# Attention sums on TensorE: products stored side by side, and matrix rows 2 and 3 summed there too

## Chip, core and metric

The kernel runs on one NeuronCore of a Trainium2 chip. The metric is the device time of one execution in microseconds (us), the median of several runs. The engines are TensorE (PE in the rows, with its weight loads apart as PEld), VectorE (DVE), ScalarE (ACT), GpSimd (POOL) and the DMA queues (SP). They work in parallel and wait for each other through semaphores.

## What is computed

An audio tower: seven 1-d convolutions with layer norm and GELU over 64 clips, a projection to 12 positions of 192 numbers a clip, one attention block and one mixture of experts. The change touches the attention alone, whose reference is, cut to what matters:

```python
sim1 = jnp.einsum('bhnd,bhmd->bhnm', q, k_landmarks)      # same for sim2, sim3
attn1 = jax.nn.softmax(sim1, axis=-1)                     # and attn2, attn3
z = jnp.swapaxes(x, -1, -2) / (jnp.max(col) * jnp.max(row))
for _ in range(iters):                                    # 6 times, x = attn2
    xz = x @ z
    z = 0.25 * z @ (13.0 * I - xz @ (15.0 * I - xz @ (7.0 * I - xz)))
out = attn1 @ (attn2_inv @ (attn3 @ v))
```

There are 64 clips x 12 heads. The 12 positions are padded to 64 landmarks; since all pads are alike the kernel keeps them as one extra row, so each head's matrix is 13 x 13 (`R` is 13, `SEQ` 12), and the iteration is rewritten so that only products of symmetric results are left, two of them an iteration.

## The kernel before

The attention puts one clip and one half of the heads on each of the 128 partitions ("lanes"): a partition holds 6 heads (`HL`) with their small matrices, so a matrix product is no TensorE matmul. It is a multiplication of a row, spread over all columns, with the other matrix (13 x 13 x 6 heads = 1014 words a partition), followed by a sum over the inner index. A `RowSums` job describes one such product and says who does which row. In order the program does: `scoring` (q times k, 16 terms a sum), softmax and norms, `valuing` (attention matrix times v, 12 terms), `outer` (13 terms), then in a hardware loop of `PINV_ITERS` = 6 iterations `squaring` and `closing` (13 terms each), and last `applying` (13 terms). A job's rows go three ways:

- `sum_pe`: VectorE multiplies them into `for_pe` (L1211) and TensorE sums them: one matmul a term, with the identity as weights, that adds into the same PSUM columns (L1037). In the trace each of these fp32 matmuls stands as two records. ScalarE copies the sums out (L1123), for the symmetric products also to the mirrored place. `sum_pe_pool` are rows that GpSimd multiplies into `pool_for_pe` (L1086) for the same treatment, in a second batch.
- `by_vector`: VectorE multiplies into `rowt` (L1225) and sums (L1229) itself.
- `by_pool`: GpSimd multiplies into `from_pool` (L1089), VectorE sums (L1233).

Symmetric products skip what the mirror gives: row i is computed from column i on, and ScalarE copies it to the column (L1118). For a loop product rows 0 and 1 are `sum_pe`, rows 2 and 3 `by_vector`, rows 4 to 12 `by_pool`. The first operand of VectorE's products is read from PSUM: rows 0 and 1 where TensorE summed them, others after ScalarE brought them there (L1135).

Each job ends in a wait of VectorE for all its row sums and copies; ScalarE's next copies and GpSimd's next products wait for the same. Between the two products of an iteration VectorE forms `c4` (L1313); GpSimd waits for it. No scheduler moves anything: each engine's order is as written.

Two other kinds of matmul matter for the prediction because of how they read: the convolutions (L562, fp32, 400 columns) read their input with a step of 2 words (8 bytes), since their stride is 2; the experts' matmuls (L1438, 384 columns, a 4-byte type that is one record a matmul) read contiguous words.

The layout in `for_pe` is by term: `p (k n)`, all columns n of term k in one run, so VectorE writes a product's inner index with a step of the batch's width (156 words for rows 0 and 1 of a 13 x 13 product) and TensorE reads each term as one contiguous run.

Of the kernel before, what the change touches and what calls it, by code (L numbers as in the profile page):

```python
# [32 lines left out]
P = 128  # L33
# [735 lines left out]
class RowSums:  # L769


    def __init__(self, terms, width, sum_pe, sum_pe_pool, by_vector, by_pool, near, first, second, out, bank=0, mirror=None):
        self.batches = [rows for rows in (sum_pe, sum_pe_pool) if rows]
        self.terms, self.width, self.bank = terms, width, bank
# [13 lines left out]
    def by_term(self, buffers, i):  # L788

        batch = next(n for n, rows in enumerate(self.batches) if i in rows)  # L790
        places, wide = self.places(self.batches[batch])
        full = buffers[batch][:, 0:self.terms * wide].rearrange("p (k n) -> p k n", k=self.terms)[:, :, places[i]]
        return full.rearrange("p k (a b) -> p a b k", a=self.first(i).shape[1])

    def copies(self, bank, rows):

        places, wide = self.places(rows)
        if self.mirror:
            last = len(rows)
            both = bank[:, 0:wide].rearrange("p (i h j) -> p i h j", i=last, h=self.first(0).shape[1])  # L800
            whole, below = self.mirror(None)
            yield whole, both.rearrange("p i h j -> p h i j")
            yield below, both[:, :, :, last:].rearrange("p i h j -> p h i j")
            return
# [6 lines left out]
    def copied(self):  # L811

        batch = list(self.sum_pe) + list(self.sum_pe_pool)
        return (2 if self.mirror else len(batch)) + len(self.mirrors())


class Before:


    def __init__(self, jobs=0, sums=0, reduced=0, copied=0, pooled=0):  # L820
        self.jobs, self.sums, self.reduced, self.copied, self.pooled = jobs, sums, reduced, copied, pooled

    def after(self, *jobs, times=1):
        add = lambda f: sum(f(j) for j in jobs)
        return Before(self.jobs + len(jobs) * times, self.sums + add(lambda j: len(j.batches)) * times, self.reduced + add(lambda j: len(j.reduced)) * times,
# [31 lines left out]
def attention(nc, io, res, top):  # L857
# [33 lines left out]
    with ExitStack() as ctx:  # L891
# [13 lines left out]
        pool_for_pe = sb("pool_for_pe", [P, 2 * HL * R * DH])  # L905
# [11 lines left out]
        wv = sb("wv", [P, HL, R, DH])  # L917
# [13 lines left out]
        mat_row = lambda x: x.rearrange("p (h k) -> p h k", k=R)  # L931
        q_near = near_rows([bank(3, 0), bank(3, 1)], 3, HL * DH, lane_row)
# [3 lines left out]
        scoring = RowSums(DH, lambda i: HL * SEQ, [0, 1], [6, 7], [2, 3, 4, 5], [8, 9, 10, 11],  # L936
# [697 lines left out]
```

## Time and profile before

| | |
|---|---|
| median of 3 runs | 1031.38 us (1031.18 to 1031.56) |
| the profiled execution | 1027.13 us, its span on the core 1025.3 us |
| convolutions | to about 550 us of the span |
| attention | about 550 to 865 us, of it the loop 673.5 to 828 us |
| experts | from 865 us on |

The profile is of one execution. A line of the timeline has its start in us from the span's start, its length in us (of the whole group when x2 or more instructions are merged), the engine, the line of the kernel, the operation with out<-in, the shape, and in brackets the idle time of the engine ahead of it with what ended it. "PEclk" or the number behind the busy times in a row by windows is TensorE's granted clock as a share of 2.4 GHz; 0.50 is 1.2 GHz.

### The profile page before, as it was taken

Reading aid. Unit: us, or ns where it says so; the run is one execution under the profiler, and the core shown is the slowest. Engines: PE = TensorE matmul, PEld = TensorE weight load, DVE = VectorE, ACT = ScalarE, POOL = GpSimd, SP = SyncE. Lnnn points to the kernel's source line nnn. Section 1 sums busy time; section 2 is a strip of 40 time slices with the busy share of each in tenths; the row PEclk is TensorE's granted clock in tenths of the full one; section 3 lists DMA queues with packets and bytes.
Section 4 is the critical chain, followed back from the end, with each engine's and each line's share of the span. In section 5 each row is a group of like instructions: output and inputs, shape, how many; then the busy total and the mean of one; then the engine's idle time right before and its main releaser. Section 6 shows DMA issues by size and latency. Waiting matters only on the chain. (4 is left out here: it accounts for less than half of the span.)

```text
span 1025.3 us, 10797 instructions
## 1 busy us (share of the span) xinstructions
PE 744.8 (73%) x3517; PEld 530.8 (52%) x3517; DVE 644.1 (63%) x1479; ACT 269.6 (26%) x463; POOL 201.4 (20%) x199
## 2 busy tenths in 40 slices
PE   0089998999799989999962570544444464899999
PEld 0036654665465645665642460444444453899965
DVE  4818566866485552455554579999999996522243
ACT  0043354334433443433221020022222211133100
POOL 2000000000000000000000055546666682033000
PEclk9999997999698988998965586766666677699999
DMA  1430500050003300000003500000000000000000
GB/s 53 70 87 20 112 1 1 1 112 20 2 0 53 68 0 1 1 1 1 1 0 91 125 1 0 0 1 0 0 0 0 0 0 1 0 1 1 1 1 23
DMA packets 22663, 21.73 MB, mean 21 GB/s; under 512 B 17036, under 2 KB 21196, under 8 KB 21388
## 3 DMA queue, kind: packets, MB, share of 16 engines
q1 hardware_dynamic: 22620, 21.20, 9.7%
q8 instruction: 22, 0.36, 0.2%
q14 instruction: 21, 0.17, 0.1%
HBM read 17.51 MB, written 3.66 MB: 21 GB/s over the span
## 5 line engine op out<-in xcount | busy, mean ns | idle before, releaser
L562 PE MATMUL ps<-h,w 128*128 128x400 f32 x720 | 290.8, 548 | 1.6 <-ACT h L630 1.5
L562 PEld LDWEIGHTS ps<-h,w 128*128 128x128 f32 x720 | 139.3, 200 | 105.9 <-issue 103.2
L1037 PE MATMUL pt<-for_pe,ident 128*128 128x156 f32 (+2 forms) x420 | 99.3, 418 | 107.8 <-DVE for_pe L1211 107.8
L1037 PEld LDWEIGHTS pt<-for_pe,ident 128*128 128x128 f32 x420 | 91.5, 280 | 115.5 <-DVE for_pe L1211 111.9
L722 DVE COPY h<-ps 128x800 f32<-128x800 f32 (+2 forms) x58 | 56.5, 975 | 94.4 <-PE ps L562 93.6
L575 PEld LDWEIGHTS ps<-averager,sq 128*100 128x100 f32 (+2 forms) x1024 | 99.5, 172 | 23.1 <-ACT sq L623 19.3
L575 PE MATMUL ps<-averager,sq 128*100 128x1 f32 (+2 forms) x1024 | 100.0, 228 | 8.9 <-ACT sq L623 8.4
L623 ACT ACTIVATE sq<-h 128x800 f32<-128x800 f32 (+2 forms) x58 | 49.8, 858 | 174.5 <-DVE h L722 174.5
L753 DVE TENSOR_TENSOR h<-h,ps 128x400 f32<-128x400 f32 (+2 forms) x116 | 60.0, 558 | 39.0 <-PE ps L591 38.9
L630 ACT ACTIVATE h<-h,lnp 128x800 f32<-128x800 f32 (+2 forms) x58 | 60.5, 1043 | 86.1 <-DVE h L753 84.4
L602 ACT ACTIVATE h<-ps,lnp 128x800 f32<-128x800 f32 x64 | 63.4, 1011 | 63.7 <-PE ps L523 63.5
L523 PE MATMUL ps<-late,w_stack 90*128 90x400 bf16 x128 | 36.2, 373 | 48.2 <-DMA late<-windows_dram 41.3
L1070 POOL MEMSET eye<- 128x169 f32 x1 | 0.2, 241 | 343.3 <-SPq L998 343.3
L1118 ACT COPY e<-e 128x60 f32<-128x60 f32 (+9 forms) x130 | 32.2, 251 | 126.2 <-DVE e L1229 102.5
L1451 PE MATMUL pf<-down_w,acts 128*128 128x192 f32 (+1 forms) x264 | 59.1, 361 | 1.9 <-DVE acts L1536 1.9
L1089 POOL TENSOR_TENSOR from_pool<-e,c 128x702 f32<-128x702 f32 (+8 forms) x54 | 50.1, 969 | 34.8 <-DVE c L1313 34.8
L1233 DVE TENSOR_REDUCE e<-from_pool 128x54 f32<-128x702 f32 (+8 forms) x117 | 55.6, 549 | 0.0
L1536 DVE TENSOR_TENSOR acts<-silu,pf 128x768 f32<-128x768 f32 x18 | 17.2, 954 | 57.5 <-ACT silu L1470 57.5
L1089 POOL TENSOR_TENSOR from_pool<-e 128x702 f32<-128x702 f32 (+8 forms) x54 | 47.7, 922 | 24.1 <-ACT e L1118 16.6
L523 PEld LDWEIGHTS ps<-late,w_stack 90*128 90x128 bf16 x128 | 11.5, 104 | 76.9 <-issue 60.1
L1451 PEld LDWEIGHTS pf<-down_w,acts 128*128 128x128 f32 (+1 forms) x264 | 39.0, 187 | 22.0 <-issue 18.9
L1545 DVE SCALAR_TENSOR_TENSOR hidden<-pf,mix,hidden 128x192 f32<-128x192 f32 x54 | 22.5, 417 | 37.1 <-PE pf L1451 36.7
(231 smaller groups left out, 1019.4 us busy)
## 6 DMA issues: line engine op xcount, KB each, us to landing
late<-windows_dram SPq DMA_DIRECT2D x24, 375.0 KB, 7.4
windows_dram<-parts SPq DMA_DIRECT2D x12, 250.0 KB, 4.8
gate_w<-in_gate_w SPq DMA_DIRECT2D x1, 1728.0 KB, 12.3
up_w<-in_up_w SPq DMA_DIRECT2D x1, 1728.0 KB, 18.1
down_w<-in_down_w SPq DMA_DIRECT2D x1, 1728.0 KB, 22.9
w<-in_w SPq DMA_DIRECT2D x1, 1024.0 KB, 5.4
xs<-in_x SPq DMA_DIRECT2D x4, 252.5 KB, 4.2
out_tokens<-hidden SPq DMA_DIRECT2D x6, 96.0 KB, 1.6
```

What stands on the lines that cost most here:

```text
L523: mm = pe.matmul(ypair[bank][:, h, 0:400], w0_stack[:, :], win[:, b * POS0 + h * 400:b * POS0 + h * 400 + 400], start=True, stop=True)
L562: mm = pe.matmul(out, w[:, L.first_tap + t, :], source(l, s, 2 * p + c, t), start=(t == 0), stop=(t == L.taps - 1))
L575: mm = pe.matmul(var_ps[0:L.w, at:at + 1], sq[:, n["var"] % 2, c, q * L.w:(q + 1) * L.w], averager[:, 0:1], start=True, stop=True)
L602: act.activation(h0[:, s, p, 0:POS0].rearrange("p (h t) -> p h t", h=2), ypair[b][:, :, 0:400], ACT.Gelu, scale=lnp[:, 0:1], bias=lnp[:, 1 ...
L623: act.activation(sq[:, n["conv"] % 2, :, 0:L.cols].rearrange("p c (b t) -> p c b t", t=L.pos), joined(l, s, p, r).rearrange("p (c b) t -> ...
L630: act.activation(both, both, ACT.Gelu, scale=lnp[:, 2 * l:2 * l + 1], bias=lnp[:, 2 * l + 1:2 * l + 2]).then_inc(gelu_done, 1)
L722: nc.vector.tensor_copy(joined(l, s, p, r).rearrange("p (c b) t -> p c b t", c=2), ypair[n["bank"]][:, :, 0:L.cols].rearrange("p c (b t) - ...
L753: nc.vector.tensor_tensor(h, h, spread[n["scale"] % 2][:, 0:L.cols].rearrange("p (b t) -> p b t", t=L.pos), ALU.mult).then_inc(scaled, 1)
L1037: mm = pe.matmul(pt[:, job.bank + n, 0:wide], ident[:, :], sum_buffers[n][:, k * wide:(k + 1) * wide], start=(k == 0), stop=(k == job.term ...
L1089: pool.tensor_tensor(pooled_row(job, i), job.first(i), job.second(i), ALU.mult).then_inc(pool_multiplied, 1)
L1233: nc.vector.tensor_reduce(job.out(i), pooled_row(job, i), AX.X, ALU.add).then_inc(row_done, 1)
L1451: mm = pe.matmul(pf[:, n % 8 // 2, (n % 2) * 512:(n % 2) * 512 + D], acts[a:b, tile, t * P:(t + 1) * P], down_w[a:b, tile, :], start=(j == ...
```

## The change

1. **Layout.** The products for TensorE are stored side by side: `p (n k)`, the k terms of one output column next to each other. VectorE and GpSimd write them in one contiguous run. TensorE's matmul for term k reads every k-th word: a step of 13 words (52 bytes) in the 13-term jobs, 12 in `valuing`, 16 in `scoring`. The number of matmuls and columns of the first batches is the same.
2. **Second batch.** In `outer`, `squaring` and `closing`, rows 2 and 3 leave `by_vector`. VectorE multiplies them (both from column 2 on, 858 words each) into `pool_for_pe`, TensorE sums them in 13 more matmuls of 132 columns into a bank of its own, and ScalarE copies them out in two copies, after the mirror copies of the last `by_pool` rows. `by_vector` is empty for these jobs.
3. **Shares.** In `scoring` row 8 and in `valuing` row 9 move from `by_pool` to `sum_pe_pool`: the second batches there are 216 columns (before 144) and 288 (before 192).
4. **Layouts of v.** ScalarE makes `v_turned`, v with the 12 positions innermost, and `wv` is kept with its 13 rows innermost, so that `valuing` and `applying` read their second operand in one run. The last subtraction (L1321) then reads `wv` with a step.
5. **Norms.** The small multiplication of `padsum` (L1277) goes; its factor is applied in a fused instruction on one word a partition, followed by one more small addition.

```diff
+    def products(self, buffers, i):
         batch = next(n for n, rows in enumerate(self.batches) if i in rows)
         places, wide = self.places(self.batches[batch])
-        full = buffers[batch][:, 0:self.terms * wide].rearrange("p (k n) -> p k n", k=self.terms)[:, :, places[i]]
-        return full.rearrange("p k (a b) -> p a b k", a=self.first(i).shape[1])
+        row = buffers[batch][:, places[i].start * self.terms:places[i].stop * self.terms]
+        return row.rearrange("p (a b k) -> p a b k", a=self.first(i).shape[1], k=self.terms)
...
-        scoring = RowSums(DH, lambda i: HL * SEQ, [0, 1], [6, 7], [2, 3, 4, 5], [8, 9, 10, 11],
+        scoring = RowSums(DH, lambda i: HL * SEQ, [[0, 1]], [6, 7, 8], [2, 3, 4, 5], [9, 10, 11],
...
-        valuing = RowSums(SEQ, lambda i: HL * DH, [0, 1, 2], [7, 8], [3, 4, 5, 6], [9, 10, 11, 12],
+        valuing = RowSums(SEQ, lambda i: HL * DH, [[0, 1, 2]], [7, 8, 9], [3, 4, 5, 6], [10, 11, 12],
...
-                          lambda i: v_l.rearrange("p j (h d) -> p h d j", d=DH), lambda i: wv[:, :, i, :])
+                          lambda i: v_turned[:, :, :, :], lambda i: wv[:, :, :, i], whole_banks)
...
-            first = lambda i: 0 if i < FULL else i
+            first = lambda i: i // FULL * FULL if i < 2 * FULL else i
...
-            return RowSums(R, lambda i: HL * (R - first(i)), [0, 1], [], [2, 3], [4, 5, 6, 7, 8, 9, 10, 11, 12],
+            return RowSums(R, lambda i: HL * (R - first(i)), [[0, 1], [2, 3]], [], [], [4, 5, 6, 7, 8, 9, 10, 11, 12],
...
                         wide = job.places(rows)[1]
+                        by_term = sum_buffers[n][:, 0:wide * job.terms].rearrange("p (n k) -> p n k", k=job.terms)
                         for k in range(job.terms):
-                            mm = pe.matmul(pt[:, job.bank + n, 0:wide], ident[:, :], sum_buffers[n][:, k * wide:(k + 1) * wide],
+                            mm = pe.matmul(job.banks(n)[:, 0:wide], ident[:, :], by_term[:, :, k],
                                            start=(k == 0), stop=(k == job.terms - 1))
...
                     mirror(job.by_vector)
-                    mirror(job.by_pool[:-4])
-                    for n, rows in enumerate(job.batches):
-                        batch(n, rows)
-                    mirror(job.by_pool[-4:])
+                    mirror(job.by_pool[:4])
+                    batch(0, job.batches[0])
+                    mirror(job.by_pool[4:])
+                    batch(1, job.batches[1])
...
+                act.copy(v_turned[:, :, :, :], v_l.rearrange("p j (h d) -> p h d j", d=DH)).then_inc(near_ready, 1)
...
-                    dve.wait_ge(near_ready, near)
-                    for i in job.sum_pe:
-                        ins = nc.vector.tensor_tensor(job.by_term(sum_buffers, i), job.near(i), job.second(i), ALU.mult)
-                    ins.then_inc(multiplied, 1)
+                    for n, rows in enumerate(job.sum_pe):
+                        dve.wait_ge(near_ready, near if n == 0 else late_near)
+                        for i in rows:
+                            ins = nc.vector.tensor_tensor(job.products(sum_buffers, i), job.near(i), job.second(i), ALU.mult)
+                        ins.then_inc(multiplied, 1)
...
-                steps.done(nc.vector.tensor_scalar(padsum[:, :], padsum[:, :], 1.0 / ROOT, None, ALU.mult))
...
-                nc.vector.tensor_scalar(norms[:, 1:2], norms[:, 1:2], scale[:, 0:1], PADS / LANDMARKS,
-                                        ALU.max, ALU.add).then_inc(peaks, 1)
+                steps.done(nc.vector.scalar_tensor_tensor(out=norms[:, 1:2], in0=scale[:, 0:1], scalar=1.0 / ROOT, in1=norms[:, 1:2],
+                                                          op0=ALU.mult, op1=ALU.max))
+                steps.settle()
+                nc.vector.tensor_scalar(norms[:, 1:2], norms[:, 1:2], PADS / LANDMARKS, None, ALU.add).then_inc(peaks, 1)
```

VectorE at the start of the loop (`e` stands for e1 and e2, shapes are output elements), before:

```order
L1309 ISA
L1211 TENSOR_TENSOR for_pe<-pt,e 128x78x13 x2
L1214 REGISTER_ALU
L1225 TENSOR_TENSOR rowt<-pt,e 128x858
L1225 TENSOR_TENSOR rowt<-pt,e 128x780
L1228 ISA
L1229 TENSOR_REDUCE e<-rowt 128x6x11
L1228 REGISTER_ALU
L1229 TENSOR_REDUCE e<-rowt 128x6x10
L1232 ISA
L1233 TENSOR_REDUCE e<-from_pool 128x6x9
```

and after:

```order
L1315 ISA
L1220 TENSOR_TENSOR for_pe<-pt,e 128x1014 x2
L1218 REGISTER_ALU
L1220 TENSOR_TENSOR pool_for_pe<-pt,e 128x858 x2
L1239 ISA
L1240 TENSOR_REDUCE e<-from_pool 128x6x9
```

The first two products are now one run of 1014 elements in place of 78 pieces of 13, the two `rowt` products have become products into `pool_for_pe`, and their two sums have left VectorE. On TensorE, the loop before (`ident` is the weights):

```order
L1051 ISA
L1037 MATMUL pt<-for_pe,ident 128x156 x13
L1032 REGISTER_ALU
L1037 MATMUL pt<-for_pe,ident 128x156 x13
L1051 REGISTER_ALU
```

and after:

```order
L1057 ISA
L1043 MATMUL pt<-for_pe,ident 128x156 x13
L1037 REGISTER_ALU
L1043 MATMUL pt<-pool_for_pe,ident 128x132 x13
L1037 REGISTER_ALU
L1043 MATMUL pt<-for_pe,ident 128x156 x13
L1037 REGISTER_ALU
L1043 MATMUL pt<-pool_for_pe,ident 128x132 x13
L1057 REGISTER_ALU
```

Each product has 13 more matmuls, of 132 columns, behind the 13 of 156.

## Rows read from the trace of the kernel before

**Rows 1.** The page: span, and busy time of the engines (share of the span)

```profile
span 1025.3 us, 10797 instructions
...
PE 744.8 (73%) x3517; PEld 530.8 (52%) x3517; DVE 644.1 (63%) x1479; ACT 269.6 (26%) x463; POOL 201.4 (20%) x199
```

**Rows 2.** Busy time by window, the loop: length, PE, PEld, DVE, ACT, POOL (count), clock, DMA, GB/s

```profile
673.50:828.00 154.50, 69.90 (x312) 67.08 (x312) 149.00 (x188) 42.60 (x164) 97.92 (x109) 0.69 0.00 0
```

**Rows 3.** Timeline, the first loop iteration: start, length, engine, line, operation, count, wait

```profile
675.22 7.96 POOL L1089 TENSOR_TENSOR from_pool<-e 128x702 f32<-128x702 f32 x9 [7.53 <-DVE e L1302]
675.25 3.94 DVE L1211 TENSOR_TENSOR for_pe<-pt,e 128x1014 f32<-128x1014 f32 x2 [0.36 <-ACT pt L1135]
...
679.24 6.71 PE L1037 MATMUL pt<-for_pe,ident 128*128 128x156 f32 x26 [6.99 <-DVE for_pe L1211]
...
682.69 4.25 DVE L1233 TENSOR_REDUCE e<-from_pool 128x54 f32<-128x702 f32 x9
...
686.04 0.57 ACT L1123 COPY e<-pt 128x156 f32<-128x156 f32 x2
686.40 0.64 ACT L1118 COPY e<-e 128x18 f32<-128x18 f32 x3
...
687.16 1.22 DVE L1313 SCALAR_TENSOR_TENSOR c<-e 128x1014 f32<-128x1014 f32 x1 [0.22 <-ACT e L1118]
688.41 3.94 DVE L1211 TENSOR_TENSOR for_pe<-pt,c 128x1014 f32<-128x1014 f32 x2
...
699.58 0.64 ACT L1118 COPY e<-e 128x18 f32<-128x18 f32 x3
...
700.80 2.06 DVE L1211 TENSOR_TENSOR for_pe<-pt,e 128x1014 f32<-128x1014 f32 x1 [0.68 <-ACT e L1118]
```

**Rows 4.** Groups by shape, 600 to 866 us: count, busy us and mean ns

```profile
L1037 PE MATMUL pt<-for_pe,ident 128*128 128x156 f32 x338 | 76.6, 411 | 87.3 <-DVE for_pe L1211 87.3
...
L1225 DVE TENSOR_TENSOR rowt<-pt,e 128x858 f32<-128x858 f32 x6 | 6.3, 1045 | 0.0
```

**Rows 5.** Timeline of TensorE: sums of the rows GpSimd multiplied for the scores, and later transposes

```profile
611.74 4.08 PE L1037 MATMUL pt<-pool_for_pe,ident 128*128 128x144 f32 x32
...
853.17 2.79 PE L1058 MATMUL pt<-ident,attn 128*96 128x128 f32 x12 [5.15 <-DVE attn L1321]
```

**Rows 6.** Timeline of TensorE in a convolution, and its busy time in the experts (L1438)

```profile
345.15 2.30 PE L562 MATMUL ps<-h,w 128*128 128x400 f32 x6
347.29 0.50 PE L523 MATMUL ps<-late,w_stack 90*128 90x400 bf16 x2
...
900.00:950.00 50.00, 50.00 (x290) 1.00 0.00 1
```

**Rows 7.** Timeline of VectorE, two sums of the same 864 words, and softmax scaling

```profile
627.42 1.05 DVE L1271 TENSOR_REDUCE den<-smat 128x72 f32<-128x864 f32 x1
628.39 1.64 DVE L1272 TENSOR_REDUCE peak<-smat 128x72 f32<-128x864 f32 x1
...
630.76 3.30 DVE L1277 TENSOR_SCALAR padsum<-padsum 128x6 f32<-128x6 f32 x1
```

**Rows 8.** Timeline of GpSimd, the same stretch

```profile
627.40 6.63 POOL L1086 TENSOR_TENSOR pool_for_pe<-smat,lanes 128x1152 f32<-128x1152 f32 x2 [11.57 <-DVE smat L1265]
```

**Rows 9.** Timeline of VectorE, first and next work of scores, values and output

```profile
601.14 4.08 DVE L1211 TENSOR_TENSOR for_pe<-pt,lanes 128x1152 f32<-128x1152 f32 x2 [0.96 <-ACT pt L1135]
...
620.55 1.05 DVE L1245 TENSOR_REDUCE peak<-scores 128x72 f32<-128x864 f32 x1
...
634.74 6.22 DVE L1211 TENSOR_TENSOR for_pe<-pt,lanes 128x1152 f32<-128x1152 f32 x3
...
659.68 0.41 DVE L1290 TENSOR_REDUCE top_norms<-pt 1x2 f32<-1x256 f32 x1
...
828.50 6.98 DVE L1211 TENSOR_TENSOR for_pe<-pt,wv 128x1248 f32<-128x1248 f32 x3 [0.88 <-ACT pt L1135]
...
851.75 1.36 DVE L1321 TENSOR_TENSOR attn<-wv,attn 128x1152 f32<-128x1152 f32 x1
```

More of the change, by code:

```diff
@@ L769, with __init__ @@
 class RowSums:
-    def __init__(self, terms, width, sum_pe, sum_pe_pool, by_vector, by_pool, near, first, second, out, bank=0, mirror=None):
-        self.batches = [rows for rows in (sum_pe, sum_pe_pool) if rows]
-        self.terms, self.width, self.bank = terms, width, bank
+    def __init__(self, terms, width, sum_pe, sum_pe_pool, by_vector, by_pool, near, first, second, out, banks, mirror=None):
+        self.batches = sum_pe + ([sum_pe_pool] if sum_pe_pool else [])
+        self.terms, self.width, self.banks = terms, width, banks
         self.sum_pe, self.sum_pe_pool, self.by_vector, self.by_pool = sum_pe, sum_pe_pool, by_vector, by_pool
@@ L798, in copies @@
         if self.mirror:
-            last = len(rows)
-            both = bank[:, 0:wide].rearrange("p (i h j) -> p i h j", i=last, h=self.first(0).shape[1])
-            whole, below = self.mirror(None)
+            both = bank[:, 0:wide].rearrange("p (i h j) -> p i h j", i=len(rows), h=self.first(0).shape[1])
+            whole, below = self.block(rows)
             yield whole, both.rearrange("p i h j -> p h i j")
-            yield below, both[:, :, :, last:].rearrange("p i h j -> p h i j")
+            yield below, both[:, :, :, len(rows):].rearrange("p i h j -> p h i j")
             return
@@ L1085, in multiply @@
                     for i in job.sum_pe_pool:
-                        pool.tensor_tensor(job.by_term(sum_buffers, i), job.first(i), job.second(i),
+                        pool.tensor_tensor(job.products(sum_buffers, i), job.first(i), job.second(i),
                                            ALU.mult).then_inc(pool_multiplied, 1)
@@ L1296, in _ @@
                 nc.vector.tensor_scalar(top_norms[:, 2:3], top_norms[:, 1:2], -1.0, None, ALU.mult).then_inc(norm_ready, 1)
[L1297 removed]
+                sums(outer, at_outer, 5, 5)
                 dve.wait_ge(scale_spread, 1)
@@ L1306, in _ @@
                 dve.wait_ge(e_ready, 1)
-                start = steps.n
-                each = len(squaring.by_vector) + len(closing.by_vector)
                 with dve.Fori(0, PINV_ITERS) as n:
-                    steps.at(start + each * n)
                     sums(squaring, at_iteration(n), NEAR0 + 2 * n, NEAR0 + 2 * n + 1)
```

56 lines of the change are left out of this document (28 added, 28 removed).

## The prediction

> **What bounds the kernel now.** I read the page first: over the whole span TensorE is busy 73% and VectorE 63% [rows 1], which says little, since the stages have different limits. The change touches only the attention, so the next view is the busy time by window. In the loop VectorE is busy 149.0 of 154.5 us, TensorE 69.9, GpSimd 97.9, ScalarE 42.6 [rows 2]: VectorE sets the pace there. Then the timeline of one iteration [rows 3]. A squaring starts at 675.25 with the two products for TensorE (3.94 us), goes on with rows 2 and 3, and ends with nine sums of GpSimd's rows at 686.94 (682.69 + 4.25). TensorE's sums run from 679.24 to 685.95, ahead of that end. ScalarE's last mirror copy ends at 687.04, and 1.37 us later (almost all of it the c4 instruction) the closing starts at 688.41; after the closing it is 0.58 us (700.22 to 700.80). So an iteration is 700.80 - 675.25 = 25.55 us, and a product about 11.8 us with what follows its last sum. What TensorE does in it is hidden now, with about 1 us to spare. That is the number to keep: any work added to TensorE in a product soon stands on the path.
>
> **What comes off VectorE.** A product written by term costs 3.94/2 = 1.97 us for 1014 words; one written side by side costs 1.045 us for 858 [rows 3, 4], by words 1.22 us for 1014, or 2.4 us for two. Rows 2 and 3 keep their products but lose their sums. So VectorE has batch 0 ready at S + 2.4 (S: start of the product) in place of S + 3.95, batch 1 at S + 4.4, and would be through with GpSimd's rows at about S + 8.6, which GpSimd itself allows (7.96 us for its nine rows [rows 3]). By VectorE alone a product would be 3 us shorter, 40 us over 13 products.
>
> **What goes onto TensorE.** A second batch of 13 matmuls (26 records) of 132 columns, behind the 26 records of 156. At full clock a record of contiguous words costs its columns only: 144 columns in 4.08/32 = 0.1275 us with the pipeline's tail, about 0.123 us without [rows 5], so 0.133 for 156 and 0.113 for 132. The batch as it is takes 76.6/13 = 5.9 us on average [rows 4] where 26 x 0.133 = 3.5 would do: the granted clock in the loop is 0.69 [rows 2], between 1.2 and 2.4 GHz, since each batch comes after an idle time (6.99 us before the one at 679.24). So the low clock costs 2.4 us a batch. Even with reads as cheap as now, a product would then need 2.4 + 26 x (0.133 + 0.113) + 2.4 + 0.6 for the copies = 11.8 us: TensorE becomes the bound of the loop, at the old length. The loop can win nothing unless the clock stays up.
>
> **The step of the reads** decides the rest. Term k is now every 13th word, and no matmul of before reads with such a step. The bounds come from these rows. A contiguous 4-byte stream costs TensorE 50/290 = 0.173 us for 384 columns, 0.45 ns a word; a step of 8 bytes, in the convolutions, (347.29 - 345.15)/6 = 0.357 us for 400, 0.89 ns a word [rows 6], a little above the 0.34 that the contiguous batch's price gives for 400 columns. So both run into the same limit, and doubling the step doubles the price: TensorE seems to pay for a stretch of memory that it opens, not for the word. How large that stretch is, these two rows don't say beyond 8 bytes. VectorE has a row with just our step: L1271 and L1272 sum the same 864 words, contiguous in 1.05 us, and in steps of 13 words in 1.64 us, 1.90 ns a word [rows 7]. If the memory is opened at one pace for both engines, four words at 0.45 ns share one opening of about 1.8 ns, two words in steps of 8 bytes share it at 0.89, and a 52-byte step has it for itself. I take twice the convolution's price, 1.78 ns a word; the lower end is 0.89 (the convolution's own), the upper 1.95 (just above VectorE's row). That gives 0.278 us a record of 156 columns, 0.235 of 132, 0.256 of 144, 0.384 of 216, 0.513 of 288, 0.342 of 192, at either clock: 156 columns at 1.2 GHz are 0.26 us anyway.
>
> The Trainium skill speaks against this edit: Advanced Engine Details and Errata, Memory Cachelines, says that SBUF has 16-byte lines and that an engine needs at least two hits on a line to hide the access. By that rule the convolution's step is the last free one and ours is not; the rows agree with the first half (0.357 us is near the free price), and no run here shows the second. It gives no price; by a doubling it would be the sum below.
>
> **The sum, at 1.78 ns.**
> - Loop: a product is 2.4 + 26 x (0.278 + 0.235) = 13.3, + 0.6 for ScalarE's two copies (0.57 now [rows 3]) = 16.3 us. An iteration is 2 x 16.3 + 1.37 + 0.58 = 34.6 us against 25.55: +9.1, six times +54.6.
> - outer is half an iteration: +4.6.
> - scoring [rows 9], now 19.4 us from 601.14 to 620.55: two products 2.6, then 32 x 0.256 + 32 x 0.384 = 20.5, copies 0.5: 23.6, +4.2. Its VectorE work falls by two cheaper products and one sum less, and that is hidden.
> - valuing, now 24.9 us (634.74 to 659.68): three products 3.9, 48 x 0.513 = 24.6, copies 0.8: 29.3, +4.4.
> - applying, now 23.2 us (828.50 to 851.75): 4.2 + 26 x (0.513 + 0.342) = 22.2, + 0.5: 26.9, +3.7.
> - L1321 reads wv with a step: 1.36 us [rows 9] for 1152 words becomes about 2.1: +0.7, on the path.
> - Norms: L1277 took 3.30 us for 6 words a partition, ending at 634.06 when GpSimd's instruction ended (627.40 + 6.63 = 634.03) [rows 7, 8]: it waited for GpSimd. It goes, but the new fused instruction also has two sources in SBUF and can wait for the next of GpSimd's instructions in the same way; by their new lengths of about 2.6 us I get +0.8, bounds -3.1 and +2.
> - The copy to v_turned costs ScalarE 1 to 2 us, hidden: ScalarE waits for TensorE's first sums. Reordered copies: hidden too.
>
> Together 54.6 + 4.6 + 4.2 + 4.4 + 3.7 + 0.7 + 0.8 = +73.0 us on the profiled 1027.13; the median of the runs is 4 us above that execution, and I put the same difference on it: 1031.38 + 73 = 1104 us. Each 0.1 ns a word is worth about 13.5 us, so 1.5 to 1.95 ns spans 1067 to 1127.
>
> **Rivals.**
> 1. *The step costs no more than 8 bytes do*, 0.89 ns a word (0.139 and 0.118 us a record). For it: VectorE is another engine, and TensorE's two prices fit an 8-byte opening as well. Then a product is 2.4 + 6.7 + 2.4 (low clock) + 0.6 = 12.1, an iteration +0.7, the loop and outer +4.3; scoring is bound by VectorE, -2.7; valuing -5.5; applying -5.0; L1321 and norms +1.5: -7.4, 1024 us. The Trainium skill has this rule for VectorE, in the Vector Engine (DVE) Microarchitecture Reference, Measured stream behaviour on trn2: full rate only in runs of two adjacent words, any hop between being free. This case's trace speaks against carrying it to TensorE, since the convolution's words are not adjacent and cost 5% over free. Faster; 17%.
> 2. *As 1, and the clock stays up*: TensorE idles only 3.5 to 4.3 us between products instead of 7. Then a product is 2.4 + 6.7 + 0.6 = 9.7 us, an iteration 21.4: loop and outer -27, the rest -14 or so: 990 us. Against it: after 5.15 us of idle time the clock is low again, 12 records of 128 columns in 2.79 us [rows 5] where the full clock would need about 1.4, and 4 us is not far from that. 3%.
> 3. *Something between*, 1.1 to 1.5 ns, 1035 to 1067 us: 6%. The point from which the change loses is about 0.95 ns.
> 4. *Worse than VectorE's row*, because TensorE reads while VectorE and GpSimd write the same memory, or reads a word twice: over 2.1 ns, over 1145 us: 3%.
> 5. *The change doesn't do what it says*: hardly, the instructions' order shows both parts.
>
> **The numbers.** The forecast 1104 us has 71% (1067 to 1135). With the cases between, a range of 1035 to 1145 holds about 8 in 10; the fast cases 1 and 2 lie outside. A measurement of this kernel tells about 0.2% from no change. Faster by more than that: 17 + 3 = 20% less the edge of case 1, 19%; within it 2%; slower 79%.
>
> **What would show it.** The mean length of TensorE's two batches in the loop: near 7.2 and 6.1 us at any clock if I am right, 5.9 and 3 if rival 1 holds. Between two products VectorE should idle for some 7 us, waiting for ScalarE's copy of batch 1, and that for TensorE. VectorE's products for TensorE should be about 1.2 us each; if they aren't, the first step is wrong. The forecast falls if the records of 156 columns stand closer than 0.2 us.

## The result, and the profile after

The changed kernel takes 1105.84 us (median of 4 runs, 1105.3 to 1107.16), the kernel before 1031.28 us beside it: a ratio of 1.0715, 95% interval 1.0679 to 1.0752. It is slower by 74.6 us. The prediction was 1104 us.

The page of the changed kernel, its span, the busy times that answer to [rows 1], and the two groups of sums by TensorE (count, busy us, mean ns of a record, idle time before them):

```profile
span 1105.3 us, 11419 instructions
...
PE 881.1 (80%) x3855; PEld 621.1 (56%) x3855; DVE 590.1 (53%) x1451; ACT 268.5 (24%) x466; POOL 189.7 (17%) x199
...
L1043 PE MATMUL pt<-for_pe,ident 128*128 128x156 f32 (+2 forms) x420 | 130.0, 481 | 62.2 <-DVE for_pe L1220 62.2
...
L1043 PE MATMUL pt<-pool_for_pe,ident 128*128 128x132 f32 (+3 forms) x420 | 113.4, 441 | 0.0
```

VectorE has 54 us less to do, TensorE 136 us more. L1037 is L1043 now, L1211 is L1220, L1233 is L1240, L1313 is L1318, ScalarE's copies L1123 and L1135 are L1130 and L1142, and the last subtraction L1321 is L1323. The busy time by window for the six iterations of the loop, which begin at 694.05 here and at 675.25 before (columns as in [rows 2]), the changed kernel:

```profile
694.05:901.52 207.47, 161.07 (x624) 140.41 (x624) 110.34 (x162) 39.42 (x164) 98.61 (x109) 0.83 0.00 0
```

and the kernel before:

```profile
675.25:828.50 153.25, 69.90 (x312) 67.08 (x312) 147.65 (x186) 42.74 (x164) 98.39 (x109) 0.69 0.00 0
```

The loop is 54.2 us longer. VectorE, busy all but 6 us of it before, now idles for 97; TensorE's share rose from 46% to 78%, and with it the granted clock from 0.69 to 0.83, which won nothing, as the next rows show. One product of the changed kernel on the timeline (the closing; compare [rows 3] from 688.41 on):

```profile
711.81 2.34 DVE L1220 TENSOR_TENSOR for_pe<-pt,c 128x1014 f32<-128x1014 f32 x2
...
714.06 2.00 DVE L1220 TENSOR_TENSOR pool_for_pe<-pt,c 128x858 f32<-128x858 f32 x2
714.20 7.42 PE L1043 MATMUL pt<-for_pe,ident 128*128 128x156 f32 x26 [4.31 <-DVE for_pe L1220]
715.98 4.66 DVE L1240 TENSOR_REDUCE e<-from_pool 128x54 f32<-128x702 f32 x9
...
721.44 6.20 PE L1043 MATMUL pt<-pool_for_pe,ident 128*128 128x132 f32 x26
...
727.68 0.52 ACT L1130 COPY e<-pt 128x132 f32<-128x132 f32 x2 [5.13 <-PE pt L1043]
728.23 0.29 ACT L1142 COPY pt<-e 128x156 f32<-128x156 f32 x1
...
728.64 2.33 DVE L1220 TENSOR_TENSOR for_pe<-pt,e 128x1014 f32<-128x1014 f32 x2 [8.01 <-ACT pt L1142]
...
731.03 7.42 PE L1043 MATMUL pt<-for_pe,ident 128*128 128x156 f32 x26 [3.38 <-DVE for_pe L1220]
```

The product is a chain: VectorE's two products 2.34 us, TensorE's two batches 7.42 and 6.20 us, end to end, ScalarE's copies, and only then the next product. VectorE has waited 8.01 us for it. In all twelve products the batches last 7.3 to 7.42 and 6.2 us, whatever the clock: from the start of the first batch to that of the second it is 7.24 us at a granted clock of 0.61 (696.44:703.68) and 7.14 us at 0.76 (869.10:876.24). Within a batch the records start 0.272 us apart for 156 columns and 0.232 for 132 (the medians); 7.24 us are 0.278 a record. From one squaring batch to the next is 34.59 us (696.44 to 731.03).

### The profile page after: what moved, and what is told of

Same layout as the page of the kernel before. It is cut to its first block and busy times, and to the rows that moved or that the text cites. A ratio compares the mean times of both kernels' runs of the same rounds, so it can differ in the third digit from the quotient of the medians.

```text
span 1105.3 us, 11419 instructions
## 1 busy us (share of the span) xinstructions
PE 881.1 (80%) x3855; PEld 621.1 (56%) x3855; DVE 590.1 (53%) x1451; ACT 268.5 (24%) x466; POOL 189.7 (17%) x199
## 5 line engine op out<-in xcount | busy, mean ns | idle before, releaser
L562 PE MATMUL ps<-h,w 128*128 128x400 f32 x720 | 293.8, 553 | 1.9 <-ACT h L630 1.8
L562 PEld LDWEIGHTS ps<-h,w 128*128 128x128 f32 x720 | 141.7, 203 | 107.3 <-issue 104.9
L1043 PE MATMUL pt<-for_pe,ident 128*128 128x156 f32 (+2 forms) x420 | 130.0, 481 | 62.2 <-DVE for_pe L1220 62.2
L1043 PEld LDWEIGHTS pt<-for_pe,ident 128*128 128x128 f32 x420 | 101.2, 265 | 88.5 <-DVE for_pe L1220 68.7
L1043 PE MATMUL pt<-pool_for_pe,ident 128*128 128x132 f32 (+3 forms) x420 | 113.4, 441 | 0.0
L1043 PEld LDWEIGHTS pt<-pool_for_pe,ident 128*128 128x128 f32 x420 | 87.2, 208 | 24.6 <-issue 12.4
L1240 DVE TENSOR_REDUCE e<-from_pool 128x54 f32<-128x702 f32 (+8 forms) x117 | 57.3, 550 | 0.6
## 6 DMA issues: line engine op xcount, KB each, us to landing
up_w<-in_up_w SPq DMA_DIRECT2D x1, 1728.0 KB, 18.2
```

Of the source, the lines that this page charges most:

```text
L562: mm = pe.matmul(out, w[:, L.first_tap + t, :], source(l, s, 2 * p + c, t), start=(t == 0), stop=(t == L.taps - 1))
L1043: mm = pe.matmul(job.banks(n)[:, 0:wide], ident[:, :], by_term[:, :, k], start=(k == 0), stop=(k == job.terms - 1))
L1240: nc.vector.tensor_reduce(job.out(i), pooled_row(job, i), AX.X, ALU.add).then_inc(row_done, 1)
```

## Experiments

The clearest split is layout against batches. There are three layouts of the products that TensorE sums (by term, side by side, in pairs), each with one batch or with two in the loop. Medians in us:

| layout of the products | TensorE reads with a step of | one batch | two batches |
|---|---|---|---|
| by term | 1 word | 1031.3 (before) | 1034.7 (e1) |
| side by side | 12, 13 or 16 words | 1024.7 (e2) | 1105.8 (the change) |
| pairs | 2 words | 1001.5 (e5, again) | 1029.6 (e6) |

The kernel before, run beside them, had medians of 1030.4 to 1031.5. The two cells that are marked "before" and "e2" have the shares and the v of the kernel before, the others have those of the changed kernel. So down the column of two batches the layout alone differs, and along the row of pairs the second batch alone; from e2 to the pairs below it the shares and v differ too. What these are worth with one batch was not run. In e1 scoring takes 18.2 us against 19.4 before, valuing 21.0 against 24.9 and applying 20.5 against 23.2, with 0.8 us more for the last subtraction: by these rows about 7 us, an estimate.

**e1: the changed kernel without its layout.** The second batch, the shares and `v_turned` stay; products are stored by term again.

```diff
-        row = buffers[batch][:, places[i].start * self.terms:places[i].stop * self.terms]
-        return row.rearrange("p (a b k) -> p a b k", a=self.first(i).shape[1], k=self.terms)
+        full = buffers[batch][:, 0:self.terms * wide].rearrange("p (k n) -> p k n", k=self.terms)[:, :, places[i]]
+        return full.rearrange("p k (a b) -> p a b k", a=self.first(i).shape[1])
...
-                        by_term = sum_buffers[n][:, 0:wide * job.terms].rearrange("p (n k) -> p n k", k=job.terms)
+                        by_term = sum_buffers[n][:, 0:wide * job.terms].rearrange("p (k n) -> p n k", k=job.terms)
```

> The changed kernel with its layout undone alone: products are stored by term again and TensorE reads each term as one run; the second batch, the turned v and the shares stay. Theory (the step of TensorE's reads costs about 1.75 ns a word, the second batch only its columns): the second batch fits behind the first at the old price, so a loop product is 3.95 us of products, 26 x (0.133 + 0.113) us of sums, 2.4 us for the low clock and 0.6 us of copies, 13.4 us, an iteration 28.8 us (34.6 in the changed kernel, 25.55 before); with valuing about 4 us and applying about 2 us shorter than before, 1046 us in all (1036 to 1056). Rival (the second batch itself is what costs, by its work or by copies that come late): still over 1085 us. The records of 156 columns should stand 0.133 us apart at full clock.

Measured: 1034.7 us (1030.3 to 1037.76), a ratio of 1.0031 (1.0005 to 1.0057). One product of its loop:

```profile
775.36 3.28 DVE L1220 TENSOR_TENSOR pool_for_pe<-pt,c 128x858 f32<-128x858 f32 x2
775.59 5.24 PE L1043 MATMUL pt<-for_pe,ident 128*128 128x156 f32 x26 [5.89 <-DVE for_pe L1220]
...
780.67 3.09 PE L1043 MATMUL pt<-pool_for_pe,ident 128*128 128x132 f32 x26
...
783.79 0.52 ACT L1130 COPY e<-pt 128x132 f32<-128x132 f32 x2 [0.95 <-PE pt L1043]
...
784.72 3.94 DVE L1220 TENSOR_TENSOR for_pe<-pt,e 128x1014 f32<-128x1014 f32 x2 [1.98 <-ACT pt L1142]
```

So 71 of the 75 us go when the layout goes. It came out 11 us below what I expected. The direction was right (the second batch alone, with short reads, doesn't pay: 27.3 us an iteration against 25.55), the size was not: I had charged 2.4 us a batch for the low clock, and here the first batch needs 5.24 to 5.39 in the later iterations where 26 records at 0.133 would need 3.5, a surcharge of 1.8 (2.0 over all twelve). The six iterations take 166.4 us (673.27 to 839.71) where 172.8 were expected: 6.4 of the 11 us. VectorE's wait is short too, 1.98 us against 8.01.

**e2: the kernel before with the new layout and nothing else.**

```diff
-        full = buffers[batch][:, 0:self.terms * wide].rearrange("p (k n) -> p k n", k=self.terms)[:, :, places[i]]
-        return full.rearrange("p k (a b) -> p a b k", a=self.first(i).shape[1])
+        row = buffers[batch][:, places[i].start * self.terms:places[i].stop * self.terms]
+        return row.rearrange("p (a b k) -> p a b k", a=self.first(i).shape[1], k=self.terms)
...
-                            mm = pe.matmul(pt[:, job.bank + n, 0:wide], ident[:, :], sum_buffers[n][:, k * wide:(k + 1) * wide],
+                            mm = pe.matmul(pt[:, job.bank + n, 0:wide], ident[:, :], by_term[:, :, k],
```

> The kernel before with the new layout alone: products side by side, read in steps of 13 words (16 in scoring, 12 in valuing), no second batch in the matrix products, no turned v. Theory: the steps cost as in the changed kernel, but with one batch they are nearly hidden. A loop product is bound by VectorE: 2.4 us for the two products, 1.9 + 1.9 for rows 2 and 3, 4.3 for GpSimd's rows, 10.5 us, while TensorE ends at 2.4 + 7.1 = 9.5 us and its copies at 10.1; an iteration about 23 us, 2 to 2.5 us less than before, -14 us in the loop; applying 6 us longer and valuing 2 us longer, since TensorE sums two batches there at the stepped price: about 1023 us (1015 to 1032). Rival (stepped reads slow the other engines' accesses too, or cost more than their records show): 1035 us or more.

Measured: 1024.67 us (1020.69 to 1029.82), a ratio of 0.9940 (0.9910 to 0.9969): faster by 0.6%. One product of its loop, and its applying batches:

```profile
725.57 7.42 PE L1038 MATMUL pt<-for_pe,ident 128*128 128x156 f32 x26 [3.75 <-DVE for_pe L1212]
...
729.09 4.28 DVE L1234 TENSOR_REDUCE e<-from_pool 128x54 f32<-128x702 f32 x9
...
733.02 0.57 ACT L1124 COPY e<-pt 128x156 f32<-128x156 f32 x2 [0.44 <-PE pt L1038]
...
822.75 13.28 PE L1038 MATMUL pt<-for_pe,ident 128*128 128x288 f32 x26 [8.33 <-DVE for_pe L1212]
835.85 8.84 PE L1038 MATMUL pt<-pool_for_pe,ident 128*128 128x192 f32 x26
```

The same 7.42 us batch as in the changed kernel lies here beside VectorE's own sums: it ends at 732.99, those at 733.37 (729.09 + 4.28). VectorE's quicker products come through, and an iteration is 23.2 us. So neither half is the culprit by itself: the layout alone gives 0.6%, the rest of the change alone costs 0.3%, both together cost 7%. The layout makes the first batch 7.42 us long (5.1 to 6.7 before) and would make a second 6.2 (3.1 in e1), and the second batch puts itself and the first on the path, where VectorE's own sums had hidden it. The long batches do stand on the path in applying (29.2 us from VectorE's first product to its last subtraction, against 23.2 before), which is where e4 begins.

**e3: the changed kernel, its sums read with a step of 2 words** instead of 12, 13 or 16, and times a matrix of noughts. The sums that TensorE makes are left out of the computation that way; instructions, columns and order are the same.

```diff
-                            mm = pe.matmul(job.banks(n)[:, 0:wide], ident[:, :], by_term[:, :, k],
+                            mm = pe.matmul(job.banks(n)[:, 0:wide], nought[:, :], sum_buffers[n][:, k % 2:k % 2 + 2 * wide - 1:2],
```

> The changed kernel, in which TensorE's matmuls for the sums read words 2 apart, 8 bytes, in place of 12 to 16 apart; the same number of matmuls, columns and waits, and everything else as in the changed kernel. The words read are not the right ones, and the weights of these matmuls are zeros so that all numbers stay finite: the sums of these rows are left out of the result. Theory: the step alone is the cost. Records of 156 columns stand about 0.139 us apart, 132 about 0.118; with 2.4 us of low clock a product is 12.1 us, an iteration 26.2, and the whole 1026 us (1015 to 1036). Rival (the side-by-side writes or a clash of buffers between engines cost it, not the reads): over 1080 us. If the clock stays up because of the shorter idle times: about 990 us.

Measured: 1018.28 us (1017.28 to 1029.25), 87.6 us under the changed kernel. Two products of its loop:

```profile
725.02 5.25 PE L1045 MATMUL pt<-for_pe,nought 128*128 128x156 f32 x26 [3.36 <-DVE for_pe L1224]
730.12 3.21 PE L1045 MATMUL pt<-pool_for_pe,nought 128*128 128x132 f32 x26
...
749.49 6.59 PE L1045 MATMUL pt<-for_pe,nought 128*128 128x156 f32 x26 [3.35 <-DVE for_pe L1224]
755.92 3.21 PE L1045 MATMUL pt<-pool_for_pe,nought 128*128 128x132 f32 x26
```

With VectorE's writes unchanged, the distance between the words that TensorE reads is worth the whole loss and more. This is the kernel that rival 1 of the prediction priced at 1024 us; it came 6 us under that. The weights of nought are not what makes the batches short: with the identity and the same step the second batch lasts 3.19 us in e6, here 3.21.

**p1: the price of a step, by itself.** A probe that leaves the whole computation out: bursts of 12 fp32 matmuls (24 records) of 156 columns by the identity, each burst from a tile of its own with one step.

```python
burst(step[s][:, :].rearrange("p (n k) -> p n k", k=s)[:, :, 0])
burst(pairs[:, :].rearrange("p (n k) -> p n k", k=26)[:, :, 0:2])
burst(odd[:, 0:N // 2 * 26].rearrange("p (n k) -> p n k", k=26)[:, :, 1:3])
```

> A small kernel that computes nothing of the reference: series of 12 fp32 matmuls (24 records) of 156 columns with the identity as weights, each series reading its own tile with another step between words: 1, 2, 3, 4, 5, 6, 8, 12, 13, 14, 16, 24 and 32 words, then pairs of adjacent words every 26 words (starting on an even and on an odd word); then steps 1, 2, 13 and 16 again while VectorE and GpSimd multiply. Theory (memory opens in stretches of 16 bytes, one in about 1.75 ns, whatever the distance): spacing of records 0.133 us at step 1, 0.138 at 2, 0.205 at 3, 0.27 from step 4 on and no more at 32; even pairs 0.137, odd pairs 0.205; no change beside the other engines. Rival A (stretches of 8 bytes, full price from 8 bytes on, but long distances cost more): 0.138 at steps 2 to 6 and rising from there to 0.27 at 13. Rival B (the price comes from the other engines' writes): about 0.138 at step 13 alone and 0.27 only beside them.

Its timeline (step of 1 word: stepb; 2: stepc; 3: stepd; 4: stepe; 5: stepf; 13: stepn; 24: stepy; 32: stepG; "pairs" are two neighbouring words every 26, "oddpairs" the same from an odd word on; the last two beside a busy VectorE and GpSimd):

```profile
42.06 3.34 PE L52 MATMUL pt<-stepb,ident 128*128 128x156 f32 x24
45.24 3.47 PE L52 MATMUL pt<-stepc,ident 128*128 128x156 f32 x24
48.55 5.17 PE L52 MATMUL pt<-stepd,ident 128*128 128x156 f32 x24
53.56 6.81 PE L52 MATMUL pt<-stepe,ident 128*128 128x156 f32 x24
60.19 6.90 PE L52 MATMUL pt<-stepf,ident 128*128 128x156 f32 x24
...
86.88 6.74 PE L52 MATMUL pt<-stepn,ident 128*128 128x156 f32 x24
...
106.24 9.61 PE L52 MATMUL pt<-stepy,ident 128*128 128x156 f32 x24
115.66 6.59 PE L52 MATMUL pt<-stepG,ident 128*128 128x156 f32 x24
122.07 3.70 PE L52 MATMUL pt<-pairs,ident 128*128 128x156 f32 x24
125.61 5.28 PE L52 MATMUL pt<-oddpairs,ident 128*128 128x156 f32 x24
...
137.09 3.47 PE L52 MATMUL pt<-stepc,ident 128*128 128x156 f32 x24
140.40 6.72 PE L52 MATMUL pt<-stepn,ident 128*128 128x156 f32 x24
```

From one burst's start to the next, by 24 records: 0.133 us a record contiguous, 0.138 in steps of 2 words, 0.209 of 3, 0.276 of 4, 0.273 of 13, 0.267 of 32. These prices fit a charge of about 1.75 ns for each 16-byte stretch opened: with 3 words to a step three quarters of the words open a new stretch (156 x 0.75 x 1.75 = 205 ns), from 4 words on every word does (273 ns), and from 4 to 16 words and at 32 it hardly matters how far the next one is (0.265 to 0.282 us a record). With 2 words to a step half of them do, 137 ns, just about what the columns take anyway. Beside a busy VectorE and GpSimd the prices are the same (3.47 and 6.72 us again), so contention, rival 4 of the prediction, had no part in it. The Trainium skill (Advanced Engine Details and Errata, Memory Cachelines) speaks of 16-byte lines and of at least two hits a line to hide the access; these rows agree, step 2 being the last with two hits. The Trainium skill (SBUF — State Buffer, Door 1: The DMA port swizzle) adds that one can stride freely up to 4 fp32 words; here 3 already cost 57% more and 4 cost double, so only 2 are nearly free (4% more).

**p2: which wide steps cost more.** Step 24 stood out in p1 with 0.393 us a record, so a second probe, which again leaves the whole computation out, asked about its neighbours.

```diff
-STEPS = [1, 2, 3, 4, 5, 6, 8, 12, 13, 14, 16, 24, 32]
+STEPS = [1, 20, 22, 23, 24, 25, 28, 40, 48]
```

> A probe that leaves the whole computation out: bursts of 12 float32 products of 156 columns by the identity, read from a tile in steps of 1, 20, 22, 23, 24, 25, 28, 40 and 48 words, then 1, 24 and 48 again beside a busy VectorE and GpSimd. It asks what made a step of 24 words cost 2.5 ns a word in the first probe, where every other step from 4 words up cost 1.70 to 1.80. If one column's cost depends on the step being a multiple of 24 (96 bytes), 48 costs 0.39 us a record too and the others 0.265 to 0.28. If it depends on a multiple of 8 words over 16, 40 and 48 cost more and 20, 22, 23, 25 and 28 don't. If it was a disturbance of that burst alone, all lie at 0.265 to 0.28.

Measured on the timeline:

```profile
60.13 8.00 PE L53 MATMUL pt<-step_twenty,ident 128*128 128x156 f32 x24
67.94 8.82 PE L53 MATMUL pt<-step_twentytwo,ident 128*128 128x156 f32 x24
...
85.53 9.63 PE L53 MATMUL pt<-step_twentyfour,ident 128*128 128x156 f32 x24
94.97 7.00 PE L53 MATMUL pt<-step_twentyfive,ident 128*128 128x156 f32 x24
...
115.98 6.53 PE L53 MATMUL pt<-step_fortyeight,ident 128*128 128x156 f32 x24
```

Steps of 20, 22, 23 and 24 words cost 0.325, 0.360, 0.373 and 0.393 us a record, 25 and 28 cost 0.284, 48 costs 0.265. 40 costs 0.307. None of the three guesses holds: it is neither multiples of 24 nor of 8 words, nor an accident, since 24 repeats at 0.393 in both probes. The price rises from 16 words (0.265 in p1) to 24 and falls back at 25. I have no mechanism for it, and it stays open. The kernel's steps (12, 13, 16) lie outside.

**e4: pairs where e2's long batches stood on the path.** One batch in the loop as in e2; scoring, valuing and applying, with the shares and the turned v of the changed kernel, store terms 2k and 2k+1 of a sum side by side, then the same two of the next sum. TensorE then reads with a step of 2 words, while VectorE and GpSimd still write runs of two.

```diff
+        even, a = self.terms // 2 * 2, x.shape[1]
+        out = buffers[batch][:, 0:even * wide].rearrange("p (k n t) -> p n k t", n=wide, t=2)[:, places[i]]
+        two = lambda z: z[:, :, :, 0:even].rearrange("p a b (k t) -> p a b k t", t=2)
+        done = [(out.rearrange("p (a b) k t -> p a b k t", a=a), two(x), two(y))]
+        if even < self.terms:
+            last = buffers[batch][:, even * wide:self.terms * wide][:, places[i]].rearrange("p (a b) -> p a b", a=a)
+            done.append((last, x[:, :, :, even], y[:, :, :, even]))
...
+        return buffers[n][:, 0:even * wide].rearrange("p (k n t) -> p k n t", n=wide, t=2)[:, k // 2, :, k % 2]
```

> Squaring loop as in e2 (one batch of two rows, products side by side, read in steps of 13 words). Scoring, valuing and applying keep the shares and the turned V of the changed kernel, but their terms lie as neighbouring pairs: terms 2k and 2k+1 of a sum side by side, then the same two of the next sum, so that TensorE reads in steps of 2 words and VectorE and GpSimd still write runs of two. Theory (a read costs about 1.75 ns for each 16-byte stretch opened, and a product written in runs of two words is as quick as one written side by side): the long batches of valuing and applying fall from 12.4 and 13.3 us to about 7, those of GpSimd's rows likewise, and the kernel gains on e2 what TensorE's rows held up there: about 1 us in scoring, 8 in valuing, 9 in applying, less 1 for the copy of V and norms. Span of the profiled run some 17 us under e2's, median 1008 us (1000 to 1018). Rival A (a run of two words is too short for VectorE's writes, which then cost what the writes by term cost, 2.0 against 1.2 us for 2028 elements): batches as short, but VectorE is later by 0.8 us a row, median 1018 or more. Rival B (VectorE's own sums end the stages, not TensorE's rows): no change against e2, 1023 to 1026.

Measured: 1001.58 us (1000.65 to 1011.93), a ratio of 0.9748 (0.9697 to 0.9798). Scoring and applying on its timeline:

```profile
603.12 2.62 DVE L1247 TENSOR_TENSOR for_pe<-pt,lanes 128x1152 f32<-128x1152 f32 x2 [0.96 <-ACT pt L1168]
...
605.80 5.95 PE L1068 MATMUL pt<-for_pe,ident 128*128 128x144 f32 x32 [4.62 <-DVE for_pe L1247]
...
807.88 4.56 DVE L1247 TENSOR_TENSOR for_pe<-pt,wv 128x1152 f32<-128x1152 f32 x6 [1.21 <-ACT pt L1168]
...
812.50 9.21 PE L1068 MATMUL pt<-for_pe,ident 128*128 128x288 f32 x26 [6.21 <-DVE for_pe L1247]
...
821.54 4.57 PE L1068 MATMUL pt<-pool_for_pe,ident 128*128 128x192 f32 x26
```

From the first product of a stage to what follows it, in us:

| | before | changed | e2 | e4 |
|---|---|---|---|---|
| scoring | 19.4 | 23.0 | 19.1 | 16.8 |
| valuing | 24.9 | 29.1 | 27.3 | 19.6 |
| applying | 23.2 | 26.7 | 29.2 | 18.8 |

The theory holds, somewhat better than priced: against e2 scoring gains 2.3 us where I expected 1, valuing 7.7 for 8, applying 10.4 for 9. Not all of it is the pairs: e2's second operands were read with a step as well (6.25 us for the three products of valuing, 3.88 with the turned v; 6.68 and 4.56 in applying), and e4 has the other shares. How the gain divides was not run. A run of two words is long enough for VectorE's writes: the two products of scoring take 2.62 us in pairs and 2.62 us side by side in the changed kernel. The Trainium skill says so of VectorE's ports (Vector Engine (DVE) Microarchitecture Reference, Measured stream behaviour on trn2: full rate in runs of two neighbouring words, any hop between them). These rows agree for writes. For TensorE's reads neighbours are not needed: a step of 2 words has none and costs 0.138 us against 0.133.

**e5: pairs in the loop too**, one batch. To e4's edit the loop's jobs add:

```diff
-                           lambda i: b[:, :, first(i):R, :], lambda i: out[:, :, i, first(i):R], lambda m: bank(n, m), mirror)
+                           lambda i: b[:, :, first(i):R, :], lambda i: out[:, :, i, first(i):R], lambda m: bank(n, m), mirror, pairs=True)
```

> e4 with the pairs in the loop and the outer product too. 13 terms make six pairs and a last term in a block of its own, so each row of a product takes a second, small instruction of 156 elements. Theory: the loop's batch falls from 7.42 us to about 4.6 (13 reads a row set, at about 0.14 to 0.17 us each, more where the clock is low), but in e2 VectorE's last sum ended 0.4 us after TensorE's batch, so VectorE is late next: the iteration stays at 23.2 us, less at most 0.5, plus 0.2 to 0.4 us a product for the added small instructions. Median within 4 us of e4, 1004 to 1014. Rival (TensorE's batch, with the ACT copies behind it, is what ends each product in e2): an iteration shorter by 3 us or more, and the median 20 us under e4's.

Measured: 1002.25 us (1000.14 to 1006.06), a ratio of 0.9729 (0.9690 to 0.9768), and beside e6 once more:

> e5 once more, on the same chip as e6, so that the two can be compared without the difference between chips: 1002 us (1000 to 1006) by every theory.

Measured: 1001.53 us (1000.74 to 1002.76), 0.9725 (0.9709 to 0.9741). The batch lasts 5.3 to 6.75 us instead of 7.42 (I had expected about 4.6, more at a low clock), and an iteration 22.9 instead of 23.2: as expected VectorE is late next, and its two small added instructions (2.56 us for four against 2.33 for two) eat part of what is won. e4 and e5 can't be told apart by their medians.

**e6: pairs with the second batch**, that is the changed kernel with pairs in place of its layout; only the storing and reading lines of e4 are added to it, and `pairs=True` in all jobs.

> The changed kernel with one thing altered: the terms of every sum lie as neighbouring pairs instead of all side by side. The second batch stays, so against e5 it differs in the second batch alone. Theory (the change's loss has two parts: reads in wide steps, and a product that cannot end before both batches have ended one after the other): with the wide steps gone the batches take about 5.9 and 3.2 us as in e5 and e1, the first starts 2.6 us into the product, and VectorE, whose own sums end before that, waits for TensorE: a product of about 12.3 us and an iteration of 24.6, 1.7 over e5's. Six iterations and the outer product give 11 us: median 1013 (1007 to 1019), between e5 and e1. Rival (TensorE, busier than in e5, is granted the high clock, and its first batch falls to 3.7 us): iteration near 21 us, median 990. Rival (nothing but the layout was wrong, and the second batch is as good as VectorE's sums): 1002, as e5.

Measured: 1029.55 us (1024.76 to 1033.56), a ratio of 0.9970 (0.9939 to 1.0001), 28 us over e5. Two batches of its loop and the next:

```profile
733.61 6.57 PE L1068 MATMUL pt<-for_pe,ident 128*128 128x156 f32 x26 [3.71 <-DVE for_pe L1247]
...
740.02 3.19 PE L1068 MATMUL pt<-pool_for_pe,ident 128*128 128x132 f32 x26
...
747.75 6.34 PE L1068 MATMUL pt<-for_pe,ident 128*128 128x156 f32 x26 [4.54 <-DVE for_pe L1247]
```

The sign was right, the size was missed by 16 us. I had put a product at 12.3 us; from 733.61 to 760.83 an iteration is 27.2, 13.6 a product. I had left out c4 (1.22 us an iteration), and from there on the first batch takes 6.3 to 6.6 us, not 5.9. The granted clock goes with it (the busy time by window, the first of these two batches in e6, of TensorE's sums alone):

```profile
733.61:740.15 6.54, 6.54 (x28) 6.54 (x29) 0.55 0.00 0
```

and in e1, the batch at 775.59:

```profile
775.59:780.80 5.21, 5.21 (x28) 5.21 (x29) 0.70 0.00 0
```

In e6 TensorE idles 3.7 to 4.5 us ahead of a batch, less than e1's 4.95 to 5.9, and still starts it at 1.2 GHz and stays there longer: the granted clock is 0.50 for the batch's first 5.0 us (733.61:738.60) against 3.0 us in e1 (775.59:778.60). What VectorE gained by writing pairs (2.56 instead of 3.94 us), the clock took back, and an iteration is 27.2 us in e6 and 27.3 in e1. Why the clock is lower in e6 the runs don't say. Against e3, which also has two batches read in steps of 2 words, e6 is 11 us slower. Its loop takes 162.7 us (677.61 to 840.35) against 156.1 (669.42 to 825.48): VectorE's products for the first batch take 0.2 us longer, and the first batches, from start to start of the next, 6.2 us on average against 5.9. But that a second batch doesn't pay even with reads at their cheapest is shown twice, most cleanly by e6 against e5.

## Why the prediction was right

- **VectorE's side.** Products side by side at 1.2 us each, 2.4 for the two: 2.33 to 2.34 us. Through with GpSimd's rows at S + 8.6: 8.8 (715.98 + 4.66 - 711.81). Idle for some 7 us between two products: 8.0. Right.
- **The price of the step** was the deciding term. Taken at 1.78 ns a word from two rows of TensorE and one of VectorE; measured 1.74 ns (0.272 us for 156 columns, 2% under the forecast's 0.278). That a word beyond the stretch pays for an opening alone was an inference from three rows, one of them another engine's; p1 measured it on TensorE, and its prices fit a stretch of 16 bytes.
- **One leg of that inference was weak.** "Doubling the step doubles the price" compared two kinds of record: 0.45 ns a word is the experts' type, one record a matmul, and 0.89 the convolutions' fp32. Contiguous fp32 already cost 0.85 ns a word in [rows 5] (0.123 us for 144 columns), so on one type the step of 2 words cost 4% more and not double, as p1 shows too (0.133 and 0.138 us). Both of TensorE's rows lay at or near the contiguous price of their own type and said nothing of a longer step. What pointed to 1.8 was VectorE's row alone, from another engine, and that twice 0.89 comes so near the measured price was partly luck.
- **The loop.** 54.6 us forecast, 54.2 measured; an iteration 34.6 against 34.59. The batches at 7.2 and 6.1 us were 7.42 and 6.20, each with a last record that overlaps what follows. The path was the one forecast: VectorE's products, two batches end to end, ScalarE's copies.
- **outer** +4.6: +5.0 (from 673.52 to 694.05, 20.5 us against 15.6).
- **scoring** +4.2: +3.6. TensorE's steps of 16 words cost 1.70 ns, less than those of 13. **valuing** +4.4: +4.2. **applying** +3.7: +3.5.
- **L1321** +0.7: +0.8 (2.14 us). **Norms** +0.8: +0.2. The step that was to be removed took 3.30 us, all but a few tenths of it waiting for GpSimd; what was forecast happened, in a smaller size. Two fused instructions take long now, one ahead of the removed step's place (0.58 us before, L1275) and the new one behind it, which ends at 644.28 together with GpSimd's products (636.85 + 7.43):

```profile
639.68 2.28 DVE L1282 SCALAR_TENSOR_TENSOR den<-smat,den 128x72 f32<-128x72 f32 x1
...
642.53 1.75 DVE L1290 SCALAR_TENSOR_TENSOR norms<-scale,norms 128x1 f32<-128x1 f32 x1
```

- **The copy to v_turned**: 2.22 us for the 1 to 2 forecast, hidden, as said.
- **The rest.** Those terms make +71.4 us (73.0 were forecast) between the two profiled executions; these differ by 80.0 (1107.16 and 1027.13). The remainder is 5.8 us by which the attention starts later and 2.7 us behind it, where nothing was changed. The medians differ by 74.6, since the execution profiled before was 4.1 us under its median. So of the median's 74.6 us some 71 are the predicted terms and about 3 are not explained by them. The start of the attention wanders between executions (601.1 to 609.9 us in the profiles of this document, with the same convolutions), so its 5.8 us need not come from the change.
- **The low clock** at 2.4 us a batch: 1.8 in e1's later iterations, 2.9 in e6's (6.5 against 26 x 0.138 = 3.6). It was right as a mean and wrong as a constant. In the changed kernel it costs next to nothing (7.24 us a batch at 0.61, 7.14 at 0.76): p1, at full clock, has the same 0.273 us for a record in steps of 13.
- **The warning that the loop can win nothing even with cheap reads** was the second argument of the prediction, and e1 and e6 bear it out. Rival 2 (the clock stays up when TensorE idles only 3.5 to 4.3 us) is refuted by e3: after 3.35 us of idle time its batches took 5.2 to 6.7 us, where 26 x 0.138 = 3.6 would have done. The granted clock in the two shown is 0.70 and 0.54, and over its loop the mean price of a low clock is about 2.4 us again.

## What to carry to other kernels

- A layout has writers and a reader. Before turning one around for the engine that is the bound, price it for the others: here a read of TensorE that opens a new 16-byte stretch for every fp32 word cost double (1.75 ns a word) and a step of 2 words next to nothing. Storing neighbours in pairs served both sides: 1029.6 us where side by side gave 1105.8, all else the same, and 1001.5 us with one batch.
- Work that is hidden has a cover, and moving the cover onto the hidden engine costs twice. The 7.42 us batch was free beside VectorE's own sums in e2 and stands whole on the path of the changed kernel. Two halves of a change that measure +0.3% and -0.6% apart lost 7% together, so time them apart and together.

## What the runs showed of the hardware

- The step between the words that TensorE reads costs by 16-byte stretches opened (p1: 0.133, 0.138, 0.209, 0.276 us a record of 156 columns at 1, 2, 3, 4 words), the same beside busy VectorE and GpSimd. In steps of 13 words the kernel's price is nearly the same at a low clock (7.24 us a batch at 0.61) as at a higher one (7.14 at 0.76). With a step of 2 words it is not: 6.54 us a batch at 0.55 in e6, 5.10 at 0.70 in e3. Two neighbouring words from an even one on share a stretch (0.148 us a record for pairs every 26 words, by burst starts); from an odd word on half of such pairs straddle two, and cost 0.213.
- Of the steps tried, those of 20 to 24 words cost the most (24 words 2.5 ns a word), with 40 next. Unexplained.
- A lower granted clock came in p2 while TensorE was busy without a gap, reading in steps of 22 to 24 words: 0.50 in the rows of step 24 (busy time by window), where steps of 13 in p1 held 1.00:

```profile
85.53:94.90 9.37, 9.37 (x25) 7.86 (x24) 0.00 (x0) 0.00 (x0) 0.50 0.00 0
```

The same step in p1 had 0.78 and cost the same 0.393 us a record, so it is the step that sets its price there, not the clock. What lowered the clock the runs don't say.
